# A bias row that moves from VectorE into the accumulated products of a graph network's relation passes

## Chip, cores, metric

One Trainium2 chip, one core of it. The metric is the device time of one execution of the whole program in microseconds (us). The kernel before takes 5387.83 us, the median of three runs.

## What is computed

Four graph networks run one after the other on 50000 node rows and 25000 edges, all of width 128 in float32, with a layer norm of the sum between them. The change lies in the second of them, the relation network, which has three layers and works on edge slots, since only nodes that are the end of an edge differ from a constant. Its reference, cut to what matters:

```python
def _cell(h_in, relv, W, b, src, dst, rel, n_nodes):
    msg = relu(h_in[src] + relv[rel])
    s = segment_sum(msg, dst)
    cnt = segment_sum(ones, dst)
    red = s / maximum(cnt, 1.0)[:, None]
    return red @ W.T + b

h = _cell(h, relvecs[0], lin_w[0], lin_b[0], ...)
for l in range(1, 3):
    h_prev = h
    _h = relu(_layer_norm(h, ln_w[l - 1], ln_b[l - 1]))
    new_h = _cell(_h, relvecs[l], lin_w[l], lin_b[l], ...)
    h = h_prev + new_h
h = _layer_norm(h, ln_w[-1], ln_b[-1])
```

So layer l + 1 needs two things of layer l: the normalized rows, which it gathers by the edges' source, and the sum h itself, to which its own product and its own bias `lin_b[l+1]` are added.

## The kernel before

The kernel is one long program of passes. A pass owns its tiles and semaphores, runs on all engines, and ends with a barrier. The three passes of the relation network are named r0, r1 and r2 here and are made by the class `RelSlots` with l = 0, 1, 2. Each works through 49 blocks of 512 edge slots (4 columns of 128 partitions).

The order on each engine is fixed by hand. A method (`sync` for SyncE or SP, which issues the plain DMAs, `gpsimd`, `tensor`, `scalar`, `vector`) returns a list of steps with a lag each. At time t an engine runs every step of its list, in list order, on block t minus its lag. The semaphore waits `done(engine, sem, b, back)` (the step of block b - back has been done) and `landed` (the DMA of block b - back has landed) stand at the head of each step, and each engine works strictly in its own order.

For a block b the work goes as follows.

- GpSimd (POOL) issues four indirect DMAs (L1695) that gather 128 source rows each into `r_G`, a ring of four blocks. It waits only for the messages of block b - 4.
- `messages` (L1708, L1711, TensorE): the kind vectors times a one-hot `r_oh` in one matmul over 512 columns, and then four matmuls of the gathered rows with a diagonal of shares, all into PSUM `r_t`. Each float32 matmul shows as two instructions.
- `relu` (L1743, ScalarE) makes `r_mT` from it.
- `run_sums` (L1605, VectorE, called DVE here): a scan over 512 columns gives the sums per destination, `r_agT`, a ring of four in r0 and r1 and of two in r2.
- `product` (L1718, TensorE): four matmuls `r_agT` times the layer's weights into PSUM `r_w`.
- `mix` (L1800 or L1802, DVE): `r_w` plus the centred bias row in r0, or plus `r_prev` (the stored sum of the pass before) in r1 and r2, gives `r_y`.
- `square` (L1750) and `deviation` (L1756) on ScalarE, `scale` (L1812), `norm` (L1818, four instructions) and `cut` (L1823) on DVE make the normalized rows `r_u`, which SP stores (L1668).
- `next_bias` (L1807, DVE) adds the next layer's centred bias row to `r_y` and writes `r_yb`, a ring of four; SP stores it as `rel_y` (L1664). The next pass loads it as `r_prev` (L1656).
- r0 has one more DVE step, `spread_shares` (L1790), which makes the diagonals of shares.

DVE's order at time t in r0 and r1 is therefore: spread_shares(t) in r0 alone, cut(t-6), mix(t-4), run_sums(t-2), next_bias(t-4), scale(t-5), norm(t-5). TensorE's order is product(t-3), messages(t-1).

The last pass, r2, stores no sum. It norms the rows, adds the rows `n_rows` (`r_xx`, L1828), norms again (L1080 to L1137), turns the result on TensorE (`turn`, L1725, lag 9), multiplies it with the next network's weights (`rows`, L1732, lag 10), and stores both: `r_nT` by `store_nT` (L1673, lag 11 on SP) and `r_res` (L1677, lag 12). ScalarE's `keep_turned` (L1767) waits for the store of `r_nT` two blocks back. The one-hot load at the head of SP's list (L1652) waits for the messages two blocks back in r2, and all later DMAs of that time stand behind it.

The bias rows `br` lie on all 128 partitions for the three layers; `one_row` is one partition of 128 ones that other passes use already.

Of the kernel before, what the change touches and what calls it, by code (L numbers as in the profile page):

```python
# [9 lines left out]
ALU = mybir.AluOpType  # L10
# [3 lines left out]
P = 128  # L14
D = 128
KT = 4
# [81 lines left out]
def spread(ap, n):  # L98

    return ap.unsqueeze(1).to_broadcast([ap.shape[0], n, ap.shape[1]])  # L100
# [13 lines left out]
def done(eng, sem, b, back=0):  # L114

    if not isinstance(b.n, int) or b.n >= back:
        eng.wait_ge(sem, b.n + (1 - back))
# [1490 lines left out]
class RelSlots(Stream):  # L1608


    def __init__(self, kn, q, l):
        self.kn, self.l, self.last = kn, l, l == 2
        self.G = q.sb("G", [P, 4, KT, D])
        self.Y = 2 if self.last else 4
        self.oh = q.sb("oh", [8, self.Y, BLOCK])
        self.mT = q.sb("mT", [P, 2, BLOCK])
        self.agT = q.sb("agT", [P, self.Y, BLOCK])
        self.y = q.sb("y", [P, self.Y, KT, D])
        self.yb = q.sb("yb", [P, 4, KT, D]) if l < 2 else None
        self.prev = q.sb("prev", [P, 4, KT, D]) if l else None  # L1620
        self.junk = q.sb("junk", [P, KT, D])
        self.ss, self.sd, self.rr = (q.sb(n, [P, 4, KT]) for n in ("ss", "sd", "rr"))
        self.pt = [q.ps(f"t{j}") for j in range(2)]
        self.pw = [q.ps(f"w{j}") for j in range(2)]
        self.gin, self.ohin, self.pin = (q.sems(n, 4) for n in ("rows_in", "kinds_in", "before_in"))
        if l < 2:
            self.stored, self.ystored = q.sems("stored", 4), q.sems("y_stored", 4)
        (self.mtm, self.mtk, self.scn, self.wm, self.shd, self.yn, self.ym, self.sq, self.sdm, self.rrd) = (
            q.sem(n) for n in ("messages_made", "messages_kept", "summed", "product_made", "shares_ready", "next_bias_added", "mixed",
                               "squares_made", "deviation_ready", "scale_ready"))  # L1630
        if self.last:
            self.parts = kn.end_norm(q)
            self.nrm = self.parts[0]["o"] = q.sb("nrm", [P, 2, KT, D])
            self.gr, self.nm = self.parts[2], self.parts[-1]
            self.e = kn.end_steps(self.parts, lambda b, k: self.y[:, b.m % self.Y, k, :], self.rr, self.ym, self.rrd, lambda n: kn.slot_at(kn.n0, kn.NP, n), None,
                                  kn.lw[:, 2, :])
            self.nT = q.sb("nT", [P, 2, BLOCK])
            self.res = q.sb("res", [P, 2, KT, D])
            self.pn, self.pr = q.ps("nt"), q.ps("r")
            self.tstored, self.rstored = q.sems("turned_stored", 4), q.sems("rows_stored", 4)  # L1640
            self.gate, self.xb, self.ntr, self.ntk, self.rm, self.rk = (
                q.sem(n) for n in ("store_gate", "x_beta", "out_turned", "out_kept", "rows_made", "rows_kept"))
        else:
            self.u = q.sb("u", [P, 4, KT, D])
            self.un, self.um = q.sem("normed"), q.sem("result_ready")

    def sync(self, sp):
        kn, l = self.kn, self.l

        def load(b):  # L1650
            done(sp, self.mtm, b, self.Y)
            sp.dma_start(self.oh[:, b.m % self.Y, :], kn.oh_d[:, bass.ds(b.n * BLOCK, BLOCK)]).then_inc(self.ohin[b.s4], 16)  # L1652

        def load_prev(b):
            done(sp, self.ym, b, 4)
            sp.dma_start(self.prev[:, b.s4], kn.slot_at(kn.ry[l - 1], 0, b.n)).then_inc(self.pin[b.s4], 16)  # L1656

        def load_x(b):
            done(sp, self.parts[3], b, 4)
            sp.dma_start(self.parts[0]["xx"][:, b.s4], kn.slot_at(kn.n0, kn.NP, b.n)).then_inc(self.parts[1][b.s4], 16)  # L1660

        def store_y(b):
            done(sp, self.yn, b)
            sp.dma_start(kn.slot_at(kn.ry[l], 0, b.n), self.yb[:, b.s4]).then_inc(self.ystored[b.s4], 16)  # L1664

        def store(b):
            done(sp, self.um, b)
            sp.dma_start(kn.slot_at(kn.rt[l + 1], 0, b.n), self.u[:, b.s4]).then_inc(self.stored[b.s4], 16)  # L1668

        def store_nT(b):  # L1670
            done(sp, self.ntk, b)
            sp.sem_inc(self.gate, 1)
            sp.dma_start(kn.hTs[0][bass.ds(b.n, 1)].rearrange("b p n -> (b p) n"), self.nT[:, b.s2, :]).then_inc(self.tstored[b.s4], 16)  # L1673

        def store_rows(b):
            done(sp, self.rk, b)
            sp.dma_start(kn.slot_at(kn.st[0], kn.NP, b.n), self.res[:, b.s2]).then_inc(self.rstored[b.s4], 16)  # L1677

        return ([(load, 0)] + ([(load_prev, 2)] if l else []) + ([(load_x, 5), (store_nT, 11), (store_rows, 12)] if self.last else
                                                               [(store_y, 8), (store, 10)]))  # L1680

    def stores_landed(self, sp):
        for s in (self.tstored, self.rstored) if self.last else (self.stored, self.ystored):
# [14 lines left out]
    def tensor(self, pe):  # L1698
        kn, l = self.kn, self.l
# [14 lines left out]
        def product(b):  # L1714
            done(pe, self.scn, b)
            done(pe, self.ym, b, 2)
            for k in range(KT):
                mm = pe.matmul(self.pw[b.s2][:, k * P:(k + 1) * P], self.agT[:, b.m % self.Y, k * P:(k + 1) * P], kn.Wr[:, l, :], start=True, stop=True)  # L1718
            mm.then_inc(self.wm, 1)

        def turn(b):
# [57 lines left out]
    def vector(self, v):  # L1779
        kn, l = self.kn, self.l  # L1780
# [11 lines left out]
        def mix(b):  # L1792
            done(v, self.wm, b)
            done(v, self.sq, b, self.Y)
            if l:
                landed(v, self.pin, b)
            done(v, self.gr if self.last else self.un, b, self.Y)
            before = self.prev[:, b.s4].rearrange("p k d -> p (k d)") if l else spread(kn.br[:, 0, :], KT)
            if l:
                v.tensor_tensor(self.y[:, b.m % self.Y].rearrange("p k d -> p (k d)"), self.pw[b.s2][:, :], before, ALU.add).then_inc(self.ym, 1)  # L1800
            else:
                v.tensor_tensor(self.y[:, b.m % self.Y], self.pw[b.s2][:, :].rearrange("p (k d) -> p k d", k=KT), before, ALU.add).then_inc(self.ym, 1)  # L1802

        def next_bias(b):
            done(v, self.ym, b)
            landed(v, self.ystored, b, 4)
            v.tensor_tensor(self.yb[:, b.s4], self.y[:, b.m % self.Y], spread(kn.br[:, l + 1, :], KT), ALU.add).then_inc(self.yn, 1)  # L1807

        def scale(b):
            done(v, self.sdm, b)  # L1810
# [23 lines left out]
        if self.last:  # L1834
            e = self.e
            return [(e["aggregate"](v), 7), (mix, 4), (e["scale2"](v), 8), (run_sums, 2), (e["shift"](v), 8), (add_x, 6), (scale, 5), (x_beta, 5),
                    (e["gamma"](v), 5), (e["stats"](v), 6)]
        return ([] if l else [(spread_shares, 0)]) + [(cut, 6), (mix, 4), (run_sums, 2), (next_bias, 4), (scale, 5), (norm, 5)]


class SageSlots(Stream):
# [1270 lines left out]
```

## Time and profile before

| | us |
|---|---|
| runs of the kernel | 5398.23, 5379.77, 5387.83 |
| median | 5387.83 |
| span of the profiled execution | 5398.9 |
| r0, from 2876 | 318 |
| r1, from 3194 | 304 |
| r2, from 3498 | 372 |

For the profiled execution no time is listed beside its span of 5398.9 us. The slowest of the three runs took 5398.23 us, so the span can be read as the whole of an execution, and it lies 11.1 us above the median. The three passes that the change touches are 994 us of it. How to read the rows: PE is a TensorE matmul, PEld its weight load, DVE is VectorE, ACT is ScalarE, POOL is GpSimd, SPq is the issue of a DMA by SyncE. A row of the timeline has the start in us from the span's start, the length in us, the engine, the line and the operation as output<-inputs, how many instructions were merged, and in brackets the idle time of the engine before it and what ended that.

### The profile page before, as it was taken

Reading aid. Unit: us, or ns where it says so; the run is one execution under the profiler, and the core shown is the slowest. Engines: PE = TensorE matmul, PEld = TensorE weight load, DVE = VectorE, ACT = ScalarE, POOL = GpSimd, SP = SyncE. Lnnn points to the kernel's source line nnn. Section 1 sums busy time; section 2 is a strip of 40 time slices with the busy share of each in tenths; the row PEclk is TensorE's granted clock in tenths of the full one; section 3 lists DMA queues with packets and bytes.
Section 4 is the critical chain, followed back from the end, with each engine's and each line's share of the span. In section 5 each row is a group of like instructions: output and inputs, shape, how many; then the busy total and the mean of one; then the engine's idle time right before and its main releaser. Section 6 shows DMA issues by size and latency. Waiting matters only on the chain. (4 is left out here: it accounts for less than half of the span.)

```text
span 5398.9 us, 104328 instructions
## 1 busy us (share of the span) xinstructions
PE 3821.1 (71%) x23663; PEld 3143.4 (58%) x23663; DVE 3792.3 (70%) x10843; ACT 3176.1 (59%) x11279; POOL 2893.9 (54%) x2759
## 2 busy tenths in 40 slices
PE   6355889566747685768575768678688787977775
PEld 5354778565537453645474545456577676866665
DVE  2575889688849784978596767677567675756666
ACT  2022889577848684868482323356577685655554
POOL 0466766603650463066205867676376564757776
PEclk8698999888979797979676767677799998988777
DMA  8898999556955694578463446555489797872221
GB/s 183 129 301 269 383 362 278 176 148 179 283 175 149 203 283 154 156 229 278 149 184 126 131 129 189 167 158 177 165 282 303 248 305 238 246 189 66 62 66 57
DMA packets 918273, 1074.23 MB, mean 199 GB/s; under 512 B 202780, under 2 KB 565066, under 8 KB 917107
## 3 DMA queue, kind: packets, MB, share of 16 engines
q1 hardware_dynamic: 763570, 890.24, 50.5%
q0 software_dynamic: 90944, 180.06, 13.6%
q10 hardware_dynamic: 63556, 1.81, 1.6%
q8 instruction: 56, 0.92, 0.1%
q14 instruction: 147, 1.20, 0.1%
HBM read 509.54 MB, written 566.14 MB: 199 GB/s over the span
## 5 line engine op out<-in xcount | busy, mean ns | idle before, releaser
L2358 POOL DMA_INDIRECT H<-gat_rows,src_i x784 | 804.1, 1026 | 1032.9 <-POOLq L79 620.9
L1909 POOL DMA_INDIRECT s_G<-sage_rows,src_i x588 | 602.4, 1025 | 369.6 <-issue 161.0
L1695 POOL DMA_INDIRECT r_G<-rel_rows,idx x392 | 441.7, 1127 | 216.8 <-issue 110.2
L1708 PE MATMUL r_t<-r_oh,relv 8*128 8x512 f32 x294 | 227.4, 862 | 217.5 <-issue 77.2
L2547 PE MATMUL p_M<-Wg,p_hT 128*128 128x132 f32 x2352 | 336.6, 287 | 63.1 <-DVE p_res L2604 48.8
L1743 ACT ACTIVATE r_mT<-r_t 128x512 f32<-128x512 f32 x147 | 87.4, 594 | 460.4 <-PE r_t L1711 460.1
L2547 PEld LDWEIGHTS p_M<-Wg,p_hT 128*128 128x128 f32 x2352 | 290.3, 192 | 113.0 <-issue 96.0
L2604 DVE SCALAR_TENSOR_TENSOR p_res<-p_M,p_rr,cg 128x132 f32<-128x132 f32 x1176 | 333.8, 346 | 2.5 <-PE p_M L2547 1.4
L1304 PE MATMUL d_S<-ones,d_sqT 128*128 128x1 f32 x1568 | 224.3, 264 | 144.0 <-DVE d_ve L1449 144.0
L2686 PEld LDWEIGHTS p_pl_p<-Wn,p_pl_h 128*128 128x128 f32 x1568 | 205.9, 198 | 201.8 <-ACT p_pl_h L2780 154.9
L2686 PE MATMUL p_pl_p<-Wn,p_pl_h 128*128 128x128 f32 x1568 | 225.3, 289 | 132.6 <-ACT p_pl_h L2780 132.4
L1304 PEld LDWEIGHTS d_S<-ones,d_sqT 128*128 128x128 f32 x1568 | 217.0, 214 | 172.2 <-issue 133.4
L1605 DVE TENSOR_TENSOR_SCAN r_agT<-same_run,r_agT,r_mT 128x512 f32<-128x512 f32 (+1 forms) x144 | 184.4, 1281 | 185.2 <-ACT r_mT L1743 185.1
L1711 PEld LDWEIGHTS r_t<-share_squares,r_G 128*128 128x128 f32 x1176 | 200.8, 258 | 160.5 <-issue 160.5
L963 POOL DMA_INDIRECT gat_rows<-early_mapv,early_mput x196 | 195.1, 995 | 168.8 <-DMA gat_rows<-early_self_map 57.6
L1695 POOL DMA_INDIRECT r_G<-n_rows,src_i x196 | 235.4, 1201 | 78.5 <-issue 54.2
L2119 POOL DMA_INDIRECT share_squares<-features,src_i x196 | 217.1, 1108 | 94.6 <-issue 58.6
L1353 ACT ACTIVATE d_hs<-d_hs,pl 128x128 f32<-128x128 f32 x784 | 248.4, 399 | 15.8 <-DMA d_hs<-gat_rows 11.9
L2406 POOL DMA_INDIRECT H<-gat_rows,dst_i x196 | 196.1, 1001 | 92.9 <-issue 48.9
L1443 DVE TENSOR_TENSOR_SCAN d_yT<-same_run,d_yT,d_T 128x512 f32<-128x512 f32 (+1 forms) x192 | 244.5, 1273 | 0.3 <-ACT d_sqT L1359 0.2
L2111 POOL DMA_INDIRECT out_dram<-tp_v,put_i x196 | 198.7, 1014 | 77.6 <-issue 56.7
L1711 PE MATMUL r_t<-share_squares,r_G 128*128 (+1 forms) x1176 | 236.6, 363 | 0.0
(482 smaller groups left out, 12286.0 us busy)
## 6 DMA issues: line engine op xcount, KB each, us to landing
gat_rows<-p_res SPq DMA_DIRECT2D x294, 264.0 KB
sage_rows<-p_pl_s SPq DMA_DIRECT2D x294, 256.0 KB
gat_rows<-x_row SPq DMA_DIRECT2D x98, 536.0 KB
gat_rows<-d_res SPq DMA_DIRECT2D x147, 264.0 KB
d_hs<-gat_rows SPq DMA_DIRECT2D x147, 256.0 KB
s_hT<-sage_slots_t SPq DMA_DIRECT2D x147, 256.0 KB
slot_rows<-H SPq DMA_DIRECT2D x49, 544.0 KB, 11.5
x_x<-in_x SPq DMA_DIRECT2D x98, 256.0 KB
```

Source lines behind the costliest of these rows:

```text
L1304: mm = pe.matmul(pS[:, k:k + 1], sqT[:, b.s2, k * P:(k + 1) * P], self.ones[:, :], start=True, stop=True)
L1353: last = act.activation(hs[:, b.s4, k, :], hs[:, b.s4, k, :], ACT.Copy, scale=self.pl[:, bass.ds(b.n * KT + k, 1)])
L1443: v.tensor_tensor_scan(yT[:, b.s4, :], self.same[:, bass.ds(b.n * BLOCK, BLOCK)], pT[b.s2][:, :], 0.0 if first else yT[:, (b.m - 1) % 4, B ...
L1695: pool.indirect_dma_start(self.G[:, g % 4, k, :], None, table, bass.IndirectOffsetOnAxis(index[:, c:c + 1], 0), bounds_check=bound, oob_is ...
L1708: pe.matmul(pt[:, :], kn.relv[:, l, :], self.oh[:, b.m % self.Y, :], start=True, stop=False)
L1711: mm = pe.matmul(pt[:, k * P:(k + 1) * P], self.G[:, b.s4, k, :], share, start=False, stop=(k == KT - 1))
L1909: pool.indirect_dma_start(self.G[:, g % 4, k, :], None, kn.st[self.l], bass.IndirectOffsetOnAxis(kn.idx[:, c:c + 1], 0), bounds_check=boun ...
L2119: pool.indirect_dma_start(self.G[:, c, :], None, kn.f, bass.IndirectOffsetOnAxis(kn.idx[:, c:c + 1], 0), bounds_check=bound, oob_is_err=Fa ...
L2358: pool.indirect_dma_start(kn.H[:, c, 0:width], None, table, bass.IndirectOffsetOnAxis(index[:, c:c + 1], 0), bounds_check=bound, oob_is_er ...
L2547: mm = pe.matmul(self.pM[self.bank(b, j)][:, k // 2, (k % 2) * TW:(k % 2 + 1) * TW], self.hT[l][:, b.s2, k * P:(k + 1) * P], kn.Wg[:, l, : ...
L2604: last = v.scalar_tensor_tensor(self.res[l][:, b.s4, k, :], self.pM[self.bank(b, j)][:, k // 2, (k % 2) * TW:(k % 2 + 1) * TW], self.rr[l] ...
L2686: mm = pe.matmul(bank[:, k * D:(k + 1) * D], xT[:, k * P:(k + 1) * P], w, start=True, stop=True)
```

## The change

DVE's step `next_bias` and its tile `r_yb` are gone. SP stores `r_y` itself, at lag 6 in place of 8, as soon as `mix` is done. Since a block of `r_y` is now read by a DMA, `mix` waits for the store of the block four back before it writes. In r1 and r2 each of the four products of a block is followed by a matmul of the row of ones with the bias row, which adds the layer's own bias into the same PSUM bank.

```diff
-        self.yb = q.sb("yb", [P, 4, KT, D]) if l < 2 else None
@@ def store_y
-            done(sp, self.yn, b)
-            sp.dma_start(kn.slot_at(kn.ry[l], 0, b.n), self.yb[:, b.s4]).then_inc(self.ystored[b.s4], 16)
+            done(sp, self.ym, b)
+            sp.dma_start(kn.slot_at(kn.ry[l], 0, b.n), self.y[:, b.s4]).then_inc(self.ystored[b.s4], 16)
@@ sync
-                                                               [(store_y, 8), (store, 10)]))
+                                                               [(store_y, 6), (store, 10)]))
@@ def product
             for k in range(KT):
-                mm = pe.matmul(self.pw[b.s2][:, k * P:(k + 1) * P], self.agT[:, b.m % self.Y, k * P:(k + 1) * P], kn.Wr[:, l, :], start=True, stop=True)
+                bank = self.pw[b.s2][:, k * P:(k + 1) * P]
+                mm = pe.matmul(bank, self.agT[:, b.m % self.Y, k * P:(k + 1) * P], kn.Wr[:, l, :], start=True, stop=(l == 0))
+                if l:
+                    mm = pe.matmul(bank, kn.one_row[0:1, :], kn.br[0:1, l, :], start=False, stop=True)
@@ def mix
             done(v, self.gr if self.last else self.un, b, self.Y)
+            if not self.last:
+                landed(v, self.ystored, b, 4)
@@ next_bias and its place in the list
-        def next_bias(b):
-            done(v, self.ym, b)
-            landed(v, self.ystored, b, 4)
-            v.tensor_tensor(self.yb[:, b.s4], self.y[:, b.m % self.Y], spread(kn.br[:, l + 1, :], KT), ALU.add).then_inc(self.yn, 1)
-
-        return ([] if l else [(spread_shares, 0)]) + [(cut, 6), (mix, 4), (run_sums, 2), (next_bias, 4), (scale, 5), (norm, 5)]
+        return ([] if l else [(spread_shares, 0)]) + [(cut, 6), (mix, 4), (run_sums, 2), (scale, 5), (norm, 5)]
```

Line numbers after L1619 are one lower in the changed kernel up to the product, whose added matmul is L1720; `mix` of r1 and r2 becomes L1804, that of r0 L1806, `norm` L1817 and `cut` L1822.

On TensorE, at the start of r1, two blocks before the change (`messages` and then `product`):

```order
L1708 MATMUL r_t<-r_oh,relv 128x512
L1711 MATMUL r_t<-share_squares,r_G 128x128 x4
L1718 MATMUL r_w<-Wr,r_agT 128x128 x4
L1708 MATMUL r_t<-r_oh,relv 128x512
L1711 MATMUL r_t<-share_squares,r_G 128x128 x4
L1718 MATMUL r_w<-Wr,r_agT 128x128 x4
```

and one block of the changed kernel at the same place:

```order
L1707 MATMUL r_t<-r_oh,relv 128x512
L1710 MATMUL r_t<-share_squares,r_G 128x128 x4
L1718 MATMUL r_w<-Wr,r_agT 128x128
L1720 MATMUL r_w<-br,one_row 128x128
L1718 MATMUL r_w<-Wr,r_agT 128x128
L1720 MATMUL r_w<-br,one_row 128x128
L1718 MATMUL r_w<-Wr,r_agT 128x128
L1720 MATMUL r_w<-br,one_row 128x128
L1718 MATMUL r_w<-Wr,r_agT 128x128
L1720 MATMUL r_w<-br,one_row 128x128
```

Four matmuls are added per block, between the four that were there, so TensorE loads weights eight times where it did four times.

On DVE, the last blocks of r0 before the change (mix, next_bias, scale, norm, cut):

```order
L1802 TENSOR_TENSOR r_y<-r_w,br 128x512
L1807 TENSOR_TENSOR r_yb<-r_y,br 128x512
L1812 RECIPROCAL r_rr<-r_sd 128x4
L1818 SCALAR_TENSOR_TENSOR r_u<-r_y,r_rr,lw 128x128 x4
L1823 TENSOR_TENSOR r_u<-r_u,nbb 128x512
L1802 TENSOR_TENSOR r_y<-r_w,br 128x512
```

The changed kernel has the same rows there without the one that writes `r_yb`; nothing else on DVE changes its order.

## Rows read from the trace of the kernel before

**Rows 1.** The windows view of r0, r1 and r2

```profile
core 0: us, PE busy (x) PEld busy (x) DVE busy (x) ACT busy (x) POOL busy (x), PEclk, DMA share, GB/s
2876.00:3194.00 318.00, 226.35 (x882) 158.70 (x882) 239.24 (x490) 97.98 (x490) 235.42 (x196) 0.70 0.39 124
3194.00:3498.00 304.00, 219.66 (x882) 154.60 (x882) 213.46 (x441) 98.31 (x490) 219.04 (x197) 0.69 0.56 172
3498.00:3870.00 372.00, 283.64 (x1414) 221.22 (x1414) 268.72 (x910) 219.97 (x807) 222.66 (x196) 0.77 0.52 168
```

**Rows 2.** The waits of r0: who waited for whom, us, times, longest

```profile
POOL r_G L1695 <- PE r_t L1711: 5.2, 17, 0.3
```

**Rows 3.** The waits of r1, same columns

```profile
POOL r_G L1695 <- PE r_t L1711: 2.4, 8, 0.3
```

**Rows 4.** The waits of SP in r1

```profile
SPq L1656 <- DVE r_y L1800: 25.0, 20, 7.5
```

**Rows 5.** The tile view of r_G: lengths in ns, min/median/max

```profile
L1695 POOL DMA_INDIRECT r_G<-rel_rows,idx x392: 993/1000/1949, 3195.1 to 3829.1; - x196
```

**Rows 6.** Timeline of r0, gathers of POOL, then DVE's operations at their starts

```profile
3069.89 1.42 POOL L1695 DMA_INDIRECT r_G<-n_rows,src_i  x1 [0.30 <-issue]
...
3073.01 1.42 POOL L1695 DMA_INDIRECT r_G<-n_rows,src_i  x1 [0.30 <-issue]
...
3069.23 1.27 DVE L1605 TENSOR_TENSOR_SCAN r_agT<-same_run,r_agT,r_mT 128x512 f32<-128x512 f32 x1
3070.42 0.67 DVE L1807 TENSOR_TENSOR r_yb<-r_y,br 128x512 f32<-128x512 f32 x1
...
3072.87 0.68 DVE L1823 TENSOR_TENSOR r_u<-r_u,nbb 128x512 f32<-128x512 f32 x1
```

**Rows 7.** Timeline of r1, a gather that starts inside next_bias

```profile
3275.96 1.41 POOL L1695 DMA_INDIRECT r_G<-rel_rows,idx  x1 [0.30 <-issue]
...
3275.83 0.66 DVE L1807 TENSOR_TENSOR r_yb<-r_y,br 128x512 f32<-128x512 f32 x1
```

**Rows 8.** Timeline of r1, a gather during which next_bias starts

```profile
3320.62 1.00 POOL L1695 DMA_INDIRECT r_G<-rel_rows,idx  x1 [0.30 <-issue]
...
3320.73 0.67 DVE L1807 TENSOR_TENSOR r_yb<-r_y,br 128x512 f32<-128x512 f32 x1
```

**Rows 9.** Lines view of r1

```profile
L1718 PE MATMUL r_w<-Wr,r_agT 128*128 128x128 f32 x392 | 75.9, 359 | 0.5 <-DVE r_agT L1605 0.5
...
L1807 DVE TENSOR_TENSOR r_yb<-r_y,br 128x512 f32<-128x512 f32 x49 | 32.7, 667 | 0.1
```

**Rows 10.** Timeline of DVE at the end of r1

```profile
3482.10 0.67 DVE L1807 TENSOR_TENSOR r_yb<-r_y,br 128x512 f32<-128x512 f32 x1
...
3488.70 0.69 DVE L1807 TENSOR_TENSOR r_yb<-r_y,br 128x512 f32<-128x512 f32 x1
```

**Rows 11.** The waits of r2

```profile
PE r_nt L1725 <- ACT r_nrm L1137: 71.1, 24, 4.4
```

**Rows 12.** Timeline of TensorE in r2

```profile
3641.33 2.08 PE L1711 MATMUL r_t<-share_squares,r_G 128*128 x8
3643.20 1.92 PE L1718 MATMUL r_w<-Wr,r_agT 128*128 128x128 f32 x8
...
3648.50 1.06 PE L1718 MATMUL r_w<-Wr,r_agT 128*128 128x128 f32 x8
3652.58 1.11 PE L1725 MATMUL r_nt<-ident,r_nrm 128*128 128x128 f32 x4 [3.02 <-ACT r_nrm L1137]
```

**Rows 13.** Timeline of SP, then of ScalarE, same stretch of r2

```profile
3643.58 0.32 SPq L1652 DMA_DIRECT2D r_oh<-kinds  x1
...
3645.35 0.36 SPq L1673 DMA_DIRECT2D sage_slots_t<-r_nT  x1
...
3648.75 0.60 ACT L1767 ACTIVATE r_nT<-r_nt 128x512 f32<-128x512 f32 x1 [4.33 <-DMA sage_slots_t<-r_nT]
...
3650.89 1.64 ACT L1137 ACTIVATE r_nrm<-r_v,r_nb,r_r 128x128 f32<-128x128 f32 x4
```

More of the change, by code:

```diff
@@ L1627, in __init__ @@
             self.stored, self.ystored = q.sems("stored", 4), q.sems("y_stored", 4)
-        (self.mtm, self.mtk, self.scn, self.wm, self.shd, self.yn, self.ym, self.sq, self.sdm, self.rrd) = (
-            q.sem(n) for n in ("messages_made", "messages_kept", "summed", "product_made", "shares_ready", "next_bias_added", "mixed",
+        (self.mtm, self.mtk, self.scn, self.wm, self.shd, self.ym, self.sq, self.sdm, self.rrd) = (
+            q.sem(n) for n in ("messages_made", "messages_kept", "summed", "product_made", "shares_ready", "mixed",
                                "squares_made", "deviation_ready", "scale_ready"))
```

## Prediction

> **What bounds the kernel now.** I read the windows view first, since the change touches three passes out of some twenty. It gives r0 318, r1 304 and r2 372 us, 994 us in all; the other 4400 us keep every instruction and cannot move. In r0 and r1 no compute engine is near its span: DVE is busy 239.24 and 213.46 us, TensorE 226.35 and 219.66 [rows 1]. POOL looks no busier, at 235.42 and 219.04 us for 196 gathers. The difference is the gap in front of each gather, 0.30 us ahead of nearly all of them, put down to issue [rows 6, 7]. So r0's gathers fill 196 x (1.20 + 0.30) = 294 of 318 us and r1's 196 x (1.12 + 0.30) = 277 of 304. The waits view says the same from the other side: POOL waited for TensorE only 5.2 us in r0 and 2.4 us in r1, never over 0.3 us at a time, which is the ordinary gap [rows 2, 3]. **r0 and r1 are POOL's**, followed by a tail of 20 to 25 us that is DVE's.
>
> r2 is different. POOL is busy 222.66 us of 372 and nobody fills the pass. The timeline shows a loop over two blocks: the messages end at 3643.4, SP issues the one-hot load that waited for them at 3643.58 and, behind it in its order, the store of `r_nT` at 3645.35; ScalarE waits 4.33 us for that store to land, writes `r_nT` at 3648.75 and ends the norm at 3652.5; TensorE, idle for 3.02 us, starts the turn at 3652.58 and comes to the next messages [rows 12, 13]. TensorE waits like that 24 times, 71.1 us in all, so 2.96 us in each loop [rows 11]. **r2 is the loop's**, and its TensorE part depends on the clock: the same eight instructions of the product take 1.92 us at 1.2 GHz and 1.06 us at 2.4 GHz [rows 12], and the granted clock was 0.77 over the pass.
>
> **The change, part by part.**
>
> *DVE loses next_bias*, 98 additions of 0.667 us [rows 9]. In the body of r0 and r1 that lies beside the gathers and is worth nothing by itself. In the tail it is on the path. After the last scan of r1 three of them run, the first at 3482.10, the last at 3488.70, in a chain in which DVE does not rest [rows 10]; the following operation starts about 0.6 us after each. So 3 x 0.6 = 1.8 us in r1, and r0's tail has the same three: **-3.6 us**.
>
> *The gathers may become shorter.* A gather takes 1.00 us at its quickest and in the median of r1 and r2 [rows 5], so r0's are stretched by 235.42 - 196 = 39 us and r1's by 219.04 - 196 = 23 us in all [rows 1]. The timeline shows by what. The gather at 3069.89 starts inside a scan that ends at 3070.50 and takes 1.42 us, so it ends 0.8 us behind the scan; that at 3073.01 starts inside the cut (3072.87 to 3073.55) and takes 1.42 [rows 6]; one that starts 0.13 us into next_bias takes 1.41 [rows 7]; but one during which next_bias starts takes 1.00 [rows 8]. A DVE operation with both inputs in SBUF that is already running when the gather starts holds it until it ends. Going through r0 in that way I find 42 gathers held by a scan (15 us), 41 held by a cut (17.5 us) and 2 held by next_bias (1 us). In r1 it is 35 by a scan (15 us), 10 by next_bias (4.6 us), none by a cut.
>
> The pattern of r0 is locked: scan, third gather behind it, cut. Without next_bias the cut moves 0.6 us forward against the scan. In the case of rows 6 it would run from 3072.28 to 3072.96 and be over when the gather starts at 3073.01. The bounds are: all 18.5 us of cut and next_bias go, or none, because a later gather falls into another operation. The scans stay either way. I take a little over half for r0, **-10 us**, since the pattern shown repeats in 41 of 49 blocks but its margin is 0.05 us. In r1 the 4.6 us go; the scan moves too, and may hold fewer or more gathers (one more in every third block, 16 x 0.4, is +6; as many fewer is -6), so r1 lies between -11 and +2: I take **-4 us**.
>
> The Trainium skill ("SBUF — State Buffer", section "Who interferes with whom") says that a tensor_tensor with two SBUF inputs contends only with GpSimd operations that read SBUF, and infers that it leaves the generation of descriptors alone. By that page this term would be zero, and the sum 14 us smaller; rows 7 speak against it.
>
> *TensorE gains four matmuls per block in r1 and r2*, eight instructions each, 128 columns like those of the product. No row shows a one-row matmul; the nearest is the product itself, so 1.06 to 1.92 us per block, on average 75.9 / 49 = 1.55 us [rows 9, 12]. Over r1 that makes 219.66 + 76 = 296 of 304 us busy at today's clock. POOL does not feel it as long as it has slack: a block's messages have to be done only when POOL comes to the same ring place, three blocks (some 16 us) later, and today it never waits. If TensorE became denser its granted clock (0.69) should rise rather than fall. Cost in r1: zero; the upper bound is under the rivals. In the tail the last product is followed by three blocks of DVE work before its mix, so zero again.
>
> In r2 two products per loop stand between the messages that release SP and the idle time before the turn: 2 x 1.06 to 2 x 1.92, so 2.1 to 3.8 us, on a cover of 2.96 us on average. I count no delay, since one of the two products already runs at 1.06 us in the loop shown. What that idle time does is of more interest. Behind 3.02 us of idleness the turn took 1.11 us for four instructions, the low clock. With one or two us left, some loops should keep the high clock. A loop whose messages run slow as at 3641.33 (2.08 us against 1.16 when fast, and as much for the one-hot part) costs about 1.9 us more. If a quarter of the 12 slow loops of r2 goes, that is **-6 us**; bounds 0 and 12 x 1.9 = -23 us.
>
> *The moved store and the added wait.* SP issues the store as soon as the mix is done, at lag 6. In r1 `load_prev` waits for that very mix just ahead of it already (25.0 us in all [rows 4]), so nothing new is queued; in r0 SP now waits there, and behind it stand the store of `r_u` and a one-hot load needed a block or more later. Mix waits for the store four blocks back, which was issued about four block times (over 16 us) earlier. next_bias waited for its own store with two blocks less, and was idle 0.1 us in all 49 cases [rows 9]. Price: zero; if that cover went, mix and the scan behind it would wait.
>
> **Sum:** -3.6 - 10 - 4 - 6 = -24 us. On the profiled execution that is 5398.9 to 5375; on the median, which is 11 us lower, **5364 us**, -0.44%. About 0.3%, 16 us, is what a measurement of this kernel can tell from no change.
>
> **Rivals.**
>
> *Nothing is released* (chance 0.27). The gathers fall into other operations and the clock stays as it is; only the tails shrink: -4 us, 5384. For it: scans hold as many gathers as cuts do, and less DVE work can move them anywhere. Against it: the margin-free 4.6 us of r1. This is also the page's rule above.
>
> *The clock of r2* (0.18). The added work fills the idle time so well that TensorE keeps 2.4 GHz in all 12 slow loops: -3.6 - 14 - 23 = -41, 5347 us. For it: every loop of r2 starts its turn slow behind an idle stretch. The Trainium skill ("TensorE: Matmul & The Clock Gate", section "What's actually happening") puts it that the throttled state is the default and activity releases it. Against: a faster TensorE opens the idle time again, since SP, the DMA and ScalarE keep their part.
>
> *TensorE becomes the bound* (0.10). If the granted clock stays at its low level through the added matmuls, they cost 1.92 us a block. r1 would need 219.66 + 49 x 1.92 = 314 us, 10 more than it has, and each loop of r2 3.84 us on 2.96 us of cover, 24 x 0.88 = +21. With the tails: 10 + 21 - 4 = +27, 5415 us. It decides once the added work of a loop exceeds the idle time in front of the turn; a mean granted clock under 0.7 in r2 would be its mark.
>
> That the change does not do what it says is not a case: the rows of the order show both halves.
>
> **How the numbers follow.** The forecast has 0.45, and a range of its own from 5350 to 5380. 8 in 10 over all cases needs the fuller clock gain and the tails alone, with some 5 us for the runs' own scatter: 5342 to 5392. Faster by over 16 us: the clock case whole and two thirds of the forecast, 0.50. Within 16 us: the rest of the forecast and nearly all of the first rival, 0.40. Slower: the last rival, 0.10.
>
> **What would show it.** Right: r0 shorter by about 12 us with POOL busy near 225 and fewer gathers of 1.42 us; r1 shorter by about 6; r2 by some 6 with shorter idle times before the turn and a granted clock over 0.77. Wrong: POOL busy unchanged in r0 (no release); POOL waiting for TensorE in r1, or DVE idle ahead of mix for the store of `r_y` (a wait that I price at zero); r2 longer than 372 us.

## Result: slower by 3.8%

The changed kernel takes 5589.89 us, the median of four runs, against 5393.03 us for the kernel before measured beside it. The ratio is 1.0376 with a 95% interval from 1.0355 to 1.0397. The forecast of 5364 us missed in sign and by far in size, and its range did not hold the time.

The span of the profiled execution is 5585.4 us, 186.5 us over that of before. Measured from the first gather of a pass to the first gather of the next, the three passes read as follows (before: 318.1, 302.1 and 399.8 us, the last with the start of the next network in it, which is why it is longer than the 372 us of [rows 1]). The windows view of the changed kernel, same columns as [rows 1]:

```profile
core 0: us, PE busy (x) PEld busy (x) DVE busy (x) ACT busy (x) POOL busy (x), PEclk, DMA share, GB/s
2879.00:3217.60 338.60, 237.25 (x882) 164.51 (x882) 210.04 (x440) 97.28 (x490) 258.74 (x197) 0.66 0.37 116
3217.60:3686.30 468.70, 451.76 (x1274) 300.32 (x1274) 189.86 (x392) 96.05 (x490) 210.43 (x196) 0.50 0.36 112
3686.30:4091.90 405.60, 378.89 (x1862) 274.06 (x1862) 272.88 (x931) 229.06 (x833) 202.46 (x196) 0.84 0.50 161
```

r0 is 20.5 us longer, r1 166.7 and r2 5.8, in all 193 us; the rest of the program is 6.5 us shorter. DVE did lose its work (189.86 us in r1 for 213.46). But TensorE is now busy 451.76 of 468.70 us in r1, and at the lowest granted clock of all, 0.50, that is at 1.2 GHz from end to end. In r0 POOL is busy 258.74 us where it was 235.43, with the same 196 gathers.

The waits of r1, who waited for whom, us, times, longest:

```profile
POOL r_G L1694 <- PE r_t L1710: 159.6, 41, 4.1
DVE r_y L1804 <- PE r_w L1720: 85.2, 49, 3.6
...
PEld r_w L1720 <- issue: 44.0, 196, 0.2
PEld r_w L1718 <- issue: 33.2, 148, 0.2
```

POOL, which waited 2.4 us before and never over 0.3 at a time [rows 3], now waits 159.6 us for the messages, up to 4.1 us at a time. And there is a kind of wait that the kernel before does not have between its products: the side of TensorE that loads weights rests for 0.2 us ahead of the load of every added matmul, and of the product behind it, seven times in a block. The timeline of TensorE in r1 shows one block:

```profile
3408.09 0.63 PE L1718 MATMUL r_w<-Wr,r_agT 128*128 128x128 f32 x2
3408.66 0.79 PE L1720 MATMUL r_w<-br,one_row 1*128 1x128 f32 x2
3409.38 0.80 PE L1718 MATMUL r_w<-Wr,r_agT 128*128 128x128 f32 x2
3410.10 0.79 PE L1720 MATMUL r_w<-br,one_row 1*128 1x128 f32 x2
3410.82 0.80 PE L1718 MATMUL r_w<-Wr,r_agT 128*128 128x128 f32 x2
...
3412.99 0.79 PE L1720 MATMUL r_w<-br,one_row 1*128 1x128 f32 x2
3413.58 1.91 PE L1707 MATMUL r_t<-r_oh,relv 8*128 8x512 f32 x2
```

Two instructions of a product and two of a bias matmul, called a pair from here on, take 1.44 us from start to start (3409.38 to 3410.82). The whole of product and bias takes from 3408.09 to 3413.58, and a block 9.2 us, where POOL would need 5.6. In r2, where the clock was 0.84, the same pairs look like this:

```profile
3805.79 0.48 PE L1720 MATMUL r_w<-br,one_row 1*128 1x128 f32 x2
3806.20 0.49 PE L1718 MATMUL r_w<-Wr,r_agT 128*128 128x128 f32 x2
3806.62 0.48 PE L1720 MATMUL r_w<-br,one_row 1*128 1x128 f32 x2
3807.03 0.49 PE L1718 MATMUL r_w<-Wr,r_agT 128*128 128x128 f32 x2
```

They take 0.83 us, and product and bias together 3.2 us per block (3805.47 to 3808.70) for what took 0.9 before. In this stretch a block of r2 is 6.75 us, TensorE without a pause.

In r0, where TensorE does nothing new, it is the gathers (POOL's, then DVE's operations at their starts):

```profile
3068.09 2.20 POOL L1694 DMA_INDIRECT r_G<-n_rows,src_i  x1 [0.30 <-issue]
...
3072.33 2.21 POOL L1694 DMA_INDIRECT r_G<-n_rows,src_i  x1 [0.30 <-issue]
...
3072.38 0.68 DVE L1792 TENSOR_TENSOR share_squares<-ident,shareD 128x512 f32 x1
3072.98 0.68 DVE L1822 TENSOR_TENSOR r_u<-r_u,nbb 128x512 f32<-128x512 f32 x1
```

The gather at 3072.33 starts 0.05 us before spread_shares (3072.38), and ends 0.88 us after the end of the cut right behind that (3073.66): it takes 2.21 us, not 1.00. 44 gathers of r0 take over 1.96 us, 51 us over the usual time together. At 43 of them spread_shares starts between 0.19 us before and 0.06 us after the gather. Before there were two, of 2.16 us each.

### The profile page after: what moved, and what is told of

It is laid out like the page before. It is cut to its first block and busy times, and to the rows that moved or that the text cites. A ratio compares the mean times of both kernels' runs of the same rounds, so it can differ in the third digit from the quotient of the medians.

```text
span 5585.4 us, 105796 instructions
## 1 busy us (share of the span) xinstructions
PE 4148.1 (74%) x24447; PEld 3341.9 (60%) x24447; DVE 3740.4 (67%) x10745; ACT 3169.4 (57%) x11279; POOL 2873.5 (51%) x2759
## 5 line engine op out<-in xcount | busy, mean ns | idle before, releaser
L1694 POOL DMA_INDIRECT r_G<-rel_rows,idx x392 | 412.9, 1053 | 411.6 <-PE r_t L1710 245.3
L1707 PE MATMUL r_t<-r_oh,relv 8*128 8x512 f32 x294 | 241.9, 915 | 152.1 <-DMA r_G<-n_rows,src_i 69.7
L1718 PE MATMUL r_w<-Wr,r_agT 128*128 128x128 f32 x1176 | 327.0, 397 | 1.1 <-DVE r_agT L1605 1.1
L1710 PEld LDWEIGHTS r_t<-share_squares,r_G 128*128 128x128 f32 x1176 | 215.7, 275 | 178.7 <-issue 178.7
L1694 POOL DMA_INDIRECT r_G<-n_rows,src_i x196 | 258.7, 1320 | 78.6 <-issue 59.1
L1718 PEld LDWEIGHTS r_w<-Wr,r_agT 128*128 128x128 f32 x1176 | 240.8, 270 | 54.7 <-issue 38.6
L1720 PE MATMUL r_w<-br,one_row 1*128 1x128 f32 x784 | 260.0, 424 | 0.0
L1710 PE MATMUL r_t<-share_squares,r_G 128*128 (+1 forms) x1176 | 253.2, 382 | 0.0
```

Source lines behind the costliest of these rows:

```text
L1694: pool.indirect_dma_start(self.G[:, g % 4, k, :], None, table, bass.IndirectOffsetOnAxis(index[:, c:c + 1], 0), bounds_check=bound, oob_is ...
L1710: mm = pe.matmul(pt[:, k * P:(k + 1) * P], self.G[:, b.s4, k, :], share, start=False, stop=(k == KT - 1))
L1718: mm = pe.matmul(bank, self.agT[:, b.m % self.Y, k * P:(k + 1) * P], kn.Wr[:, l, :], start=True, stop=(l == 0))
L1720: mm = pe.matmul(bank, kn.one_row[0:1, :], kn.br[0:1, l, :], start=False, stop=True)
```

## The experiments

Each kernel is told by its difference from the changed kernel or from that before. e5 and e6 were run four times each, beside seven runs of the kernel before, which also stand beside e7 and e8; all other times are one run beside one of the kernel before on the same chip. The kernel before took 5393 us beside the first four and 5362 or 5367 beside the others, so a time is compared only within its row. The seven runs spread over 22 us, and a difference of ten or twenty microseconds between single runs says little; the passes, read from the profiles, say more. All of them stand in this table (first gather to first gather, the granted clock of r1 and r2 in brackets):

```text
kernel                                     time   before   r0      r1            r2
before                                     5393            318.1   302.1 (0.69)  399.8 (0.75)
change                                     5590   5393     338.6   468.7 (0.50)  405.6 (0.84)
e1  no bias matmul                         5404   5393     341.4   291.4 (0.73)  398.5 (0.75)
e2  four one-row matmuls grouped           5525   5393     344.1   409.7 (0.50)  405.1 (0.75)
e3  128 rows                               5358   5393     343.8   291.2 (0.83)  362.7 (0.90)
e4  before + one-row matmuls               5562   5393     318.4   468.6 (0.50)  402.0 (0.85)
e5  128 rows, shares moved                 5305   5362     299.3   298.5 (0.85)  363.0 (0.90)
e6  as e5, bias in one matmul              5307   5362     297.9   297.1 (0.84)  369.1 (0.89)
e7  no bias matmul, useless next_bias      5359   5362     318.9   296.8 (0.70)  395.1 (0.75)
e8  before + 128-row matmuls               5338   5362     317.8   302.2 (0.81)  365.1 (0.89)
e9  64 rows                                5481   5367     345.3   371.9 (0.69)  402.9 (0.86)
e10 32 rows                                5567   5367     341.6   468.7 (0.50)  409.9 (0.83)
e11 one row, one matmul of 512 columns     5497   5367     342.9   409.6 (0.50)  395.3 (0.79)
e12 before, shares moved                   5351   5367     297.6   301.7 (0.68)  400.6 (0.75)
```

**The theories.** Theory: two causes without a common part. In r1 and r2 the one-row matmuls make TensorE the bound, since each change between one row and 128 rows makes it wait, and since the clock stays low. In r0 DVE's operations meet the gathers in a worse place. Rival: the moved store and the new wait in mix hold the passes.

### The two halves apart

e1 takes the added matmul out again and leaves the rest of the change:

```diff
-                if l:
-                    mm = pe.matmul(bank, kn.one_row[0:1, :], kn.br[0:1, l, :], start=False, stop=True)
```

> The changed kernel without the added matmuls (the bias of the second and third relation layer is left out): the DVE and SP half of the change alone. Theory (the added matmuls cost r1 its time, and r0 has a cause of its own on DVE and POOL): r1 returns to 295 to 304 us and r2 to 365 to 372, r0 stays near 338 us with POOL busy near 259; in all about 5400. Rival (the store moved to lag 6 and the new wait in mix hold the passes): r1 stays over 400 us.

e4 puts only that matmul into the kernel before:

```diff
-                mm = pe.matmul(self.pw[b.s2][...], self.agT[...], kn.Wr[:, l, :], start=True, stop=True)
+                bank = self.pw[b.s2][...]
+                mm = pe.matmul(bank, self.agT[...], kn.Wr[:, l, :], start=True, stop=(l == 0))
+                if l:
+                    mm = pe.matmul(bank, kn.one_row[0:1, :], kn.br[0:1, l, :], start=False, stop=True)
```

> The kernel before with the added one-row matmuls alone, next_bias kept (so the bias of layers two and three is added twice). Theory: r0 stays at 318 us, r1 goes to 450 to 475, r2 to 375 to 385, in all about 5560. Rival (the loss needs the removed next_bias or the moved store): r1 below 350.

e1 took 5403.9 us against 5393.1, with r0 at 341.4, r1 at 291.4 and r2 at 398.5 us. e4 took 5562.4 us, with r0 at 318.4, r1 at 468.6 and r2 at 402.0. So the matmuls alone make r1 what it is, to a tenth of a microsecond, and the DVE half alone makes r0 longer, by 23 us, and r1 shorter, by 11 us. The rival is out for r1 and r2. Both expectations missed in r2, by 27 and 17 us (365 to 372 and 375 to 385 expected); they fit the 372 us of [rows 1] and not the 399.8 up to the later boundary. r1 of e1 is also 4 us under its range. The halves cost 11 and 169 us, together 180 of the 197; the 11 us by which the DVE half shortens r1 are hidden under TensorE once both are in.

### What in the matmul costs: the changes of the row count

e2 keeps the four one-row matmuls but puts them together ahead of the products, so that the row count changes twice per block and not eight times:

```diff
-                mm = pe.matmul(bank, self.agT[...], kn.Wr[:, l, :], start=True, stop=(l == 0))
                 if l:
-                    mm = pe.matmul(bank, kn.one_row[0:1, :], kn.br[0:1, l, :], start=False, stop=True)
+                    mm = pe.matmul(self.pw[b.s2][...], kn.one_row[0:1, :], kn.br[0:1, l, :], start=(k == 0), stop=False)
+            for k in range(KT):
+                mm = pe.matmul(self.pw[b.s2][...], self.agT[...], kn.Wr[:, l, :], start=(l == 0), stop=(l == 0 or k == KT - 1))
```

> The changed kernel with the four one-row matmuls of a block together ahead of the four products, so that TensorE changes between one row and 128 rows twice per block and not eight times. Theory (each change of the row count costs, 0.36 us per instruction against 0.2 at the low clock): product and bias together take about 3.6 us at the low clock in place of 5.85, a block 7.4 in place of 9.2, and r1 lies between 300 us (if the clock rises) and 370. Rival (the one-row matmul is itself slow, or the low clock comes from the amount of work): a block still takes about 9 us, r1 450 to 470.

e3 keeps places, order and count, but sums 128 equal bias rows with a tile of 1/128, so that every matmul has 128 rows:

```diff
+            self.avg = keep("avg", [P, P])
+                v.memset(self.avg[:, :], 1.0 / P)
-                    mm = pe.matmul(bank, kn.one_row[0:1, :], kn.br[0:1, l, :], start=False, stop=True)
+                    mm = pe.matmul(bank, kn.avg[:, :], kn.br[:, l, :], start=False, stop=True)
```

> The changed kernel with the one-row matmul replaced by a full one in the same places: a 128 x 128 tile of 1/128 times all 128 equal bias rows. Same count and order of instructions, no change of the row count. Theory of the changes between row counts: a pair takes about 0.4 us at the low clock and 0.22 at the high, no gap ahead of a weight load, r1 300 to 360 us with a granted clock above 0.6. Rival (alternating between two accumulating products or two stationary tiles is the cost): r1 450 to 470 us at 0.50.

The timeline of TensorE in r1, first of e2, one block:

```profile
3406.61 2.07 PE L1718 MATMUL r_w<-br,one_row 1*128 1x128 f32 x8
3408.61 2.08 PE L1720 MATMUL r_w<-Wr,r_agT 128*128 128x128 f32 x8
3410.62 2.07 PE L1707 MATMUL r_t<-r_oh,relv 8*128 8x512 f32 x2
```

and of e3, two pairs, and one at the low clock:

```profile
3305.06 0.39 PE L1720 MATMUL r_w<-Wr,r_agT 128*128 128x128 f32 x2
3305.28 0.39 PE L1722 MATMUL r_w<-br,avg 128*128 128x128 f32 x2
3305.51 0.39 PE L1720 MATMUL r_w<-Wr,r_agT 128*128 128x128 f32 x2
3305.73 0.39 PE L1722 MATMUL r_w<-br,avg 128*128 128x128 f32 x2
...
3318.53 0.63 PE L1720 MATMUL r_w<-Wr,r_agT 128*128 128x128 f32 x2
3318.95 0.64 PE L1722 MATMUL r_w<-br,avg 128*128 128x128 f32 x2
3319.38 0.63 PE L1720 MATMUL r_w<-Wr,r_agT 128*128 128x128 f32 x2
```

In e2 the eight one-row instructions take 2.0 us from start to start and the eight of the product as much, without a gap: 4.0 us for what took 5.5 in the change, where the theory had 3.6. In e3 a pair takes 0.45 us (3305.06 to 3305.51), where the one-row pair takes 0.83 at the same clock, though nothing but the rows differs. (The 0.22 and 0.4 us that were expected are half of it, the time of one matmul and not of a pair, and r1 came out 9 us under its range.) The two runs exclude each other's rival: one-row matmuls side by side are no slower than full ones, and full ones in the same alternation have no wait. So it is the change of the row count that costs, 0.38 us per pair, which holds two changes, at 2.4 GHz; at 1.2 GHz a pair takes 1.44 us against 0.85 in e3 (3318.53 to 3319.38), so 0.59. Neither alternating between two weight tiles nor accumulating costs anything. The waits of r1 in e2 say the same by their count:

```profile
PEld r_w L1720 <- issue: 11.0, 49, 0.2
PEld r_w L1718 <- issue: 11.0, 49, 0.2
```

Two such rests per block, one at each change, where the changed kernel had seven; e3 has none on `r_w`.

The trace of before had this price in it. A change of row count happens there twice per block, into the one-hot matmul of 8 rows (L1708) and out of it. TensorE in r2 of before, at 2.4 GHz:

```profile
3655.33 1.14 PE L1708 MATMUL r_t<-r_oh,relv 8*128 8x512 f32 x2
...
3657.39 1.06 PE L1718 MATMUL r_w<-Wr,r_agT 128*128 128x128 f32 x8
3658.29 0.60 PE L1725 MATMUL r_nt<-ident,r_nrm 128*128 128x128 f32 x4
3658.72 1.06 PE L1732 MATMUL r_r<-Wn,r_nT 128*128 128x128 f32 x8
3659.71 1.12 PE L1708 MATMUL r_t<-r_oh,relv 8*128 8x512 f32 x2
3660.76 1.16 PE L1711 MATMUL r_t<-share_squares,r_G 128*128 x8
3661.76 1.06 PE L1718 MATMUL r_w<-Wr,r_agT 128*128 128x128 f32 x8
```

Eight instructions with full rows on both sides take 0.90 us (3657.39 to 3658.29). Those ahead of the one-hot matmul take 0.99 and those behind it 1.00, and the one-hot matmul itself 1.05, where a matmul of 512 columns and 128 rows takes 0.86 (e6, 3304.42 to 3305.28). The three differences make 0.38 us, the price of a pair.

The waits of r1 of before list this place too, and those of e6 show how such a row is to be read (its bias is one matmul of 512 columns and 128 rows, L1719, ahead of the products, L1721):

```profile
PEld r_t L1711 <- issue: 54.7, 49, 1.5
```

```profile
PEld r_w L1721 <- issue: 30.0, 98, 0.5
```

The 1.5 us are rest of the weight-load side, 0.76 us at 2.4 GHz, and not time lost: behind 512 columns it rests for up to 0.5 us even where the rows do not change. What differs is the overlap. With equal rows the load runs under the matmul before it, and its own matmul starts 0.43 us later; behind the 8 rows both start together. Before, and then e6:

```profile
3304.79 0.97 PEld L1711 LDWEIGHTS r_t<-share_squares,r_G 128*128 128x128 f32 x8 [0.76 <-issue]
3304.79 1.16 PE L1711 MATMUL r_t<-share_squares,r_G 128*128 x8
```

```profile
3304.42 1.02 PE L1719 MATMUL r_w<-br,avg 128*128 128x512 f32 x2
3304.85 0.19 PEld L1721 LDWEIGHTS r_w<-Wr,r_agT 128*128 128x128 f32 x1 [0.24 <-issue]
3305.28 1.05 PE L1721 MATMUL r_w<-Wr,r_agT 128*128 128x128 f32 x8
```

### What in the matmul costs: the clock

e2 was expected between 300 and 370 us in r1 and took 409.7, outside. The windows view of its r1, and of e3's r1 and r2:

```profile
3214.50:3624.20 409.70, 392.73 (x1274) 285.98 (x1274) 189.32 (x392) 96.04 (x490) 210.66 (x197) 0.50 0.41 128
```

```profile
3206.60:3497.80 291.20, 232.29 (x1274) 180.57 (x1274) 185.58 (x392) 96.95 (x490) 210.87 (x196) 0.83 0.58 180
3497.80:3860.50 362.70, 289.21 (x1862) 234.23 (x1862) 271.07 (x931) 230.22 (x833) 219.74 (x197) 0.90 0.56 180
```

In e2 TensorE never rests in the body of r1 (four groups of 2.0 us, 8.0 us per block) and yet the granted clock is 0.50. In e3 it rests between blocks, and the clock is 0.83. So it is not a full queue that brings the clock up here. The number of rows was changed alone in e9 (here) and e10 (32 in place of 64); the tile holds 1/64 or 1/32:

```diff
-                    mm = pe.matmul(bank, kn.one_row[0:1, :], kn.br[0:1, l, :], start=False, stop=True)
+                    mm = pe.matmul(bank, kn.avg[0:64, :], kn.br[0:64, l, :], start=False, stop=True)
```

> The changed kernel with the bias matmul over 64 rows (64 x 128 tile of 1/64 times 64 equal bias rows), interleaved as in the change. Theory A (every change of the row count makes TensorE wait, and the rows in use raise the clock): a pair of product and bias takes about 0.83 us at the high clock as with one row, but the clock comes up in r1, so a block there takes about 5.6 to 6.7 us and r1 290 to 340. Theory B (the number of rows does not matter to the clock, only that all are 128): r1 about 468 at 0.50.

> The same with 32 rows. Theory A: same 0.83 us per pair at the high clock, and a clock between those of one row (0.50 in r1) and of 64 rows, so r1 between 340 and 468. Theory B: as one row, r1 about 468 at 0.50.

```profile
3204.00:3575.90 371.90, 354.92 (x1274) 248.02 (x1274) 188.90 (x392) 96.05 (x490) 211.09 (x196) 0.69 0.44 141
```

```profile
3189.90:3658.60 468.70, 451.77 (x1274) 300.35 (x1274) 189.98 (x392) 95.98 (x490) 210.27 (x197) 0.50 0.36 112
```

With 64 rows the clock of r1 rises to 0.69 and r1 takes 371.9 us (a pair still takes 0.83 us at the high clock: 64 rows against 128 are a change too). With 32 rows nothing differs from one row: 468.7 us at 0.50. The expectation of something between missed for 32 rows, and r1 with 64 rows took more than the 290 to 340 us expected. In e11 the bias goes in by one one-row matmul of 512 columns:

```diff
+            if l:
+                pe.matmul(self.pw[b.s2][...], kn.one_row[0:1, :], spread(kn.br[0:1, l, :], KT), start=True, stop=False)
```

> The changed kernel with the four one-row matmuls of a block replaced by one of 512 columns ahead of the products: two changes of the row count per block, eight weight loads fewer by six. Theory (it is the one row that keeps the clock low, not the number of instructions): as with the grouped four, about 8.0 us per block of r1, r1 400 to 410 at 0.50. Rival (fewer instructions are enough): r1 under 350.

It took 409.6 us at 0.50 in r1, the same as the four grouped ones in e2 (409.7), with six instructions and six weight loads fewer per block, so the count of instructions does not matter here. But one row does not keep the clock down everywhere: the changed kernel's r2 has the same pairs and runs at 0.84, with the full matmuls of `turn` and `rows` beside them. What decides stays open. By this, r1's 469 us are two things at once. At 2.4 GHz a block with alternating rows would take 5.3 us on TensorE (1.05 + 1.0 + 3.2, an estimate from r2's rows), which POOL's 5.6 us would have hidden; at 1.2 GHz it takes 9.2.

The Trainium skill ("TensorE: Matmul & The Clock Gate", section "What's actually happening") says that the chip sets the clock by how busy TensorE has recently been. r2 of e3 agrees: it has more matmuls than before and 0.90 for 0.75. r1 of e2 does not, if busy means instructions in flight: 392.73 of 409.70 us busy, and 0.50.

### The clock by itself

e8 puts the 128-row matmuls into the kernel before, with next_bias kept:

```diff
+                if l:
+                    mm = pe.matmul(bank, kn.avg[:, :], kn.br[:, l, :], start=False, stop=True)
```

> The kernel before with 128-row bias matmuls added and next_bias kept (the bias of layers two and three is added twice). Theory (r2 gains because full matmuls keep TensorE at 2.4 GHz, whatever DVE does): r0 318, r1 300 to 305, r2 from 400 to 360 to 366 us with a granted clock near 0.9, in all about 5350. Rival (r2 gains by the removed DVE work of r0 and r1, or by something else of the change): r2 stays near 400.

r2 fell from 399.8 to 365.1 us and the time to 5337.9 against 5361.6 (about 5350 expected), with r0 and r1 unmoved. The kernel does more and does nothing less, and is quicker by 24 us, 8 us under the quickest of the seven runs of before: TensorE's added full matmuls keep the clock up (0.89) in the loop that bounds r2. The trace of before is of an earlier run than the 5361.6 us; e7, run beside e8 and with r2's instructions as before, has r2 at 395.1 us, so the gain is 30 to 35 us.

### r0

e7 is e1 with next_bias's addition put back into DVE's order, without its wait for the store, though nobody reads what it writes:

```diff
+            v.tensor_tensor(self.yb[:, b.s4], self.y[:, b.m % self.Y], spread(kn.br[:, l + 1, :], KT), ALU.add)
```

> The changed kernel without the added matmuls (the bias of layers two and three is left out), with the addition of next_bias put back on DVE in its old place though nothing reads its result. Theory (r0 lost time by the new spacing of DVE's operations against the gathers, not by any wait): r0 back from 341 to 315 to 322 us, POOL busy 235, so useless work makes it quicker; r1 from 291 to 298 to 303. Rival (store at lag 6 or the wait in mix): r0 stays above 335.

```profile
2849.10:3168.00 318.90, 244.27 (x882) 170.31 (x882) 239.15 (x489) 97.17 (x490) 236.03 (x196) 0.63 0.38 124
```

r0 is back at 318.9 us and POOL's busy time at 236.03. The store at lag 6 and the wait in mix are in e7 too, so they cost nothing that r0 shows. What next_bias did in r0 was to keep spread_shares away from the starts of gathers: none is over 1.96 us in e7, and 43 start inside the cut again and take 1.42 us, as before. r1 of e7 is 296.8 us, 1 us under its range. e5 keeps next_bias out and moves spread_shares, on the kernel e3:

```diff
-        return ([] if l else [(spread_shares, 0)]) + [(cut, 6), (mix, 4), (run_sums, 2), (scale, 5), (norm, 5)]
+        return [(cut, 6), (mix, 4), (run_sums, 2)] + ([] if l else [(spread_shares, 0)]) + [(scale, 5), (norm, 5)]
```

> The kernel with the 128-row bias matmuls, and in r0 DVE makes the diagonals of shares right behind the scan, where next_bias stood, not ahead of the cut. Theory (r0 lost 20 to 25 us because a gather that starts with spread_shares is held until the cut behind it ends, 1.2 us, about once per block): r0 falls from 344 to between 295 and 315 us, r1 and r2 stay at 291 and 363, in all 5310 to 5330. Rival (r0 is longer because of the store moved ahead on SP or the wait in mix): r0 stays above 335, in all 5355.

e6 is the same with the bias in one matmul of 512 columns:

> As the kernel with 128-row bias matmuls and the shares moved, but the bias goes in by one matmul of 512 columns ahead of the four products in place of four of 128. Same columns, six instructions fewer per block. Theory: within 5 us of the other, r1 about 291, r2 355 to 370. Rival (the interleaving of the two stationary tiles costs): r2 shorter by 10 us or more.

```profile
2861.70:3161.00 299.30, 229.43 (x882) 159.77 (x882) 212.85 (x440) 97.64 (x490) 218.21 (x197) 0.69 0.41 132
```

e5 has r0 at 299.3 us with POOL busy 218.21, and a time of 5305.05 us, ratio 0.9896 (0.9877 to 0.9915) to the kernel before. e6 has 5306.80 us, ratio 0.9898 (0.9879 to 0.9918): the two do not differ. Both have r1 at 297 to 299 us where 291 was expected, and e5's time is 5 us under its range.

e12 makes the same move in the kernel before, where next_bias stands behind it:

> The kernel before with nothing changed but that r0's spread_shares stands between the scan and next_bias in DVE's order. Theory (the place of each DVE operation against the gathers sets POOL's time): by the starts worked out from the trace the third gather behind a scan still meets the cut, so r0 stays within 310 to 325 us, while r1 and r2 do not move. If r0 falls to 300 as in the kernel without next_bias, the move of the shares alone is what pays.

```profile
2853.80:3151.40 297.60, 225.10 (x882) 158.76 (x882) 242.76 (x489) 98.00 (x490) 216.53 (x197) 0.69 0.41 133
```

The expectation missed. I had worked out from the starts that the third gather behind a scan would still meet the cut, and r0 fell to 297.6 us (5351.5 against 5367.2 in all). So with the shares moved r0 is some 20 us shorter than before, with next_bias or without. The move itself is worth 20 us with next_bias and 44 without (343.8 to 299.3, e3 to e5). Of the 39 us that r0's gathers were stretched by, 20 remain (POOL 216.53 us less 197 gathers of 1.0).

## Why the prediction was wrong, step by step

- *What bounds the kernel*: right. r0 and r1 were POOL's, and r2 the loop's through ScalarE's wait for the store, whose TensorE part depends on the clock: e8 shortens r2 by 30 to 35 us with nothing but added matmuls, at 0.89 for 0.75.
- *DVE loses next_bias, -3.6 us in the tails*, and *-4 us for r1's gathers*: right in sign and too small. r1 of e1 is 10.7 us shorter (forecast 1.8 + 4), and 6.5 of them are POOL's busy time (218.11 to 211.66). How much of it is next_bias stays open: e7, which has it again, took 296.8 us in r1 and not 302, and e5, whose r1 has the instructions of e3's 291.2 us, took 298.5. r1 moves by some 7 us with what stands ahead of it.
- *-10 us for r0's gathers*: this step failed in sign, +20.5 us measured (e1: +23.3). Its rule, that only an operation already running holds a gather, was read from a pair of rows about next_bias [rows 8]. With spread_shares starting 0.05 us after the gather and the cut behind it, the gather takes 2.21 us. The trace of before has two gathers like that in r0, of 2.16 us each, which the list of held gathers leaves out; the range should have reached to one in every block. I had moved the cut against the third gather and not spread_shares against the second.
- *Four matmuls per block, 1.06 to 1.92 us*: this step failed most. Side by side the instructions do take the time of the product's, as forecast (e2); the changes of the row count between them were put at nothing. Measured: product and bias 3.2 us per block at 2.4 GHz and 5.5 at 1.2, for 0.9 and 1.85 of the product alone, so an addition of 2.3 to 3.6 us. The rows that would have told it, the groups around the 8-row matmul of before, were not read as the price of a change of rows.
- *"its granted clock (0.69) should rise rather than fall"*: wrong for r1, where it fell to 0.50 although TensorE was busy 96% of the pass. With 128 rows it does rise, to 0.83 (e3). At 1.2 GHz throughout, a block takes 9.2 us on TensorE, more than POOL's 5.6, and the price of "zero" in r1 became 166 us. The slack of three blocks that was counted on covers a late block, not a TensorE that is slower in every one.
- *-6 us in r2 by the clock*: the clock rose (0.75 to 0.84), but a block's TensorE work grew to 6.75 us and became the bound; +5.8 us. With full rows the gain is 37 us, six times what I had counted and more than the 23 us I had set as its bound. I had counted loops whose messages run slow, but the turn and `rows` run slow more often: at 1.2 GHz they take 2.75 us together (3652.58 [rows 12] to 3655.33), at 2.4 GHz 1.42 (3658.29 to 3659.71), and the turn is slow in 28 of 49 blocks before and in 6 of e3, `rows` in 25 and 8. That is some 25 us by estimate, as far as it lies on the path; no run tests it by itself.
- *Moved store and added wait, zero*: right as far as r0 shows (e7, 318.9 us for 318.1).
- The rival *TensorE becomes the bound* named the place and the mark, a low clock that stays through the added matmuls, and had the price at +27 us instead of some +170 in r1 and r2, since it used the product's own duration as the upper end of the price of a matmul that no row of before showed.

## What to carry to other kernels

An operation moved to an idle engine is priced by what it does to its neighbours there, not by its own length: a matmul with few rows among full ones made TensorE wait at every change, and one that fills all 128 rows did the same sum with no wait. If a small addend must go into PSUM, give it all rows; putting the short ones together saved only a third of the loss (5525 us in e2, 131 over before). When an engine shares something with POOL, taking an operation away moves all the later ones against the gathers; look at which operation comes next to a gather's start, and try its place before anything else: here that alone took 20 us off r0 (e12).

## What the hardware did that I had not expected

- TensorE was at 1.2 GHz throughout r1, busy 452 of 469 us, with added matmuls of 1 or 32 rows (granted clock 0.50), but at 0.69 with 64 rows and 0.83 with 128, all else equal. The same one-row pairs ran at 0.84 in r2. No run tells what the chip looks at to decide this.
- A matmul of 512 columns and one row costs the same in a block as four of 128 side by side (409.6 and 409.7 us for r1).
- Where the row count changes between two matmuls, the weight load no longer runs under the matmul ahead of it: a change costs 0.19 us at 2.4 GHz with 1, 8 or 64 rows against 128, and 0.3 us at 1.2 GHz with one row.
- Added work that is useless to the result made a pass quicker twice: full matmuls in r2 (e8, 365.1 us, for 395 to 400) and a DVE addition in r0 (e7, 318.9 for 341.4 us).
- A gather that starts 0.05 us before spread_shares ends 0.88 us after the cut behind it, 2.21 us in all. Why next_bias, starting 0.11 us behind a gather's start [rows 8], does not hold it, while spread_shares at 0.05 us does, stays open; no run was made for it.
